# A gated cross-attention block with a quantised MLP on one Trainium2 core: an opening in four statistics groups, with four tiles normalised by GpSimd, and batch 1's tiles moved eight pieces later

## What is computed

```python
def xattn(features, textual_features, q_masks, Ws, W, w, b, Wcw, Wcb):
    txt_proj = einsum('btd,de->bte', textual_features, Ws)
    feat_proj = einsum('bfd,de->bfe', features, W)
    h = tanh(txt_proj[:, None, :, :] + feat_proj[:, :, None, :] + b)    # 2 x 2048 x 77 x 512
    rho = einsum('bftd,d->bft', h, w[:, 0]) + (1 - qm)[:, None, :] * NEG
    att = softmax(rho, axis=-1)
    txt_h = einsum('bft,btd->bfd', att, textual_features)
    return tanh(txt_h @ Wcw.T + bcw) * features + tanh(txt_h @ Wcb.T + bcb)

x = x + tanh(g_xattn) * xattn(layernorm(x), ...)
x = x + tanh(g_ffn) * ffn(layernorm(x), ...)     # silu(gate) * up, then down, operands quantised to 8 bits
```

## Time and profile before

| | us |
|---|---|
| median of 3 runs | 1372.93 (1372.75 to 1377.57) |
| profiled execution, its own time | 1375.13 |
| profiled execution, span from first to last instruction | 1373.2 |
| ACT busy | 1245.0 (91%) |
| DVE busy | 1166.2 (85%) |
| PE busy | 1117.5 (81%) |
| POOL busy | 14.0 (1%) |

### The profile page before, as it was taken

One profiled execution on the slowest core, in us unless ns is written; L12 is line 12 of the kernel. 1 busy time (PEld: TensorE's weight loads), 2 busy tenths in 40 slices (PEclk: granted clock), 3 DMA queues, 4 the chain that ended last, 5 costly groups with the idle time before them and its releaser, 6 DMA issues.

```text
span 1373.2 us, 16916 instructions
## 1 busy us (share of the span) xinstructions
PE 1117.5 (81%) x6941; PEld 353.4 (26%) x6963; DVE 1166.2 (85%) x1668; ACT 1245.0 (91%) x456; POOL 14.0 (1%) x32
## 2 busy tenths in 40 slices
PE   6888778788656787679889798787677779999998
PEld 5321112112111121112122122121111135444443
DVE  7688899986999889687999888777899967888776
ACT  4899999999899999999999999999999976555695
POOL 4000000000000000000000000000000000000000
PEclk9999899999899999899999999999998889999999
DMA  6000011100110001000000100000000004733196
GB/s 224 1 16 1 32 47 54 54 16 16 32 45 24 23 16 35 2 1 1 0 22 21 44 1 1 1 0 0 1 1 0 1 1 133 228 81 85 58 354 221
DMA packets 45107, 65.13 MB, mean 47 GB/s; under 512 B 19004, under 2 KB 21068, under 8 KB 45030
## 3 DMA queue, kind: packets, MB, share of 16 engines
q1 hardware_dynamic: 44128, 63.72, 14.6%
q10 hardware_dynamic: 197, 0.32, 0.1%
q0 software_dynamic: 704, 0.01, 0.0%
HBM read 46.20 MB, written 14.16 MB: 44 GB/s over the span
## 4 chain that ended last, share of the span: by engine, by line
ACT 76%; PE 19%; DVE 3%; DMA 1%; issue 1%; SPq 0%; DVEq 0%
ACT big L534 75%; PE ps L1241 10%; PE ps L1258 6%; PE ps L1047 1%; DMA wgu<-in_x_dram 1%; DVE big L733 1%; PE ps L1060 0%; ACT big L490 0%; PE ps L1218 0%; PE ps L1036 0%; PE ps L1104 0%; PE ps L1109 0%; DVE big L991 0%; SPq L336 0%; ACT big L527 0%
## 5 line engine op out<-in xcount | busy, mean ns | idle before, releaser
L534 ACT ACTIVATE big<-big 128x6144 f32<-128x6144 f32 x204 | 1056.7, 5268 | 5.8 <-DVE big L733 5.8
L733 DVE TENSOR_SCALAR big<-big,atxt 128x1536 f32<-128x1536 f32 (+2 forms) x915 | 794.1, 922 | 120.2 <-PE ps L1104 115.8
L1104 PE MATMUL ps<-big,wslide 128*32 128x512 f32 x4312 | 607.6, 621 | 193.8 <-ACT big L534 187.4
L1104 PEld LDWEIGHTS ps<-big,wslide 128*32 128x32 f32 x4312 | 131.5, 112 | 613.0 <-ACT big L534 318.6
L1047 PE MATMUL ps<-big,aux 128*128 128x512 f32 x256 | 144.9, 654 | 2.5 <-ACT big L476 1.6
L1241 PE MATMUL ps<-aux,wgu 128*128 128x512 bf16 x666 | 146.2, 379 | 0.7
L1109 PE MATMUL ps<-big,wslide 128*32 128x512 f32 x616 | 91.6, 710 | 39.3 <-ACT big L534 39.3
L579 ACT ACTIVATE aux<-ps,sgux 128x512 f32<-128x512 f32 x88 | 60.4, 687 | 69.0 <-PE ps L1241 66.3
L1241 PEld LDWEIGHTS ps<-aux,wgu 128*128 128x128 bf16 x680 | 66.4, 98 | 80.2 <-DMA aux<-aux 0.5
L991 DVE SCALAR_TENSOR_TENSOR big<-ps,sgux,aux 128x512 f32<-128x512 f32 x88 | 66.0, 750 | 17.8 <-PE ps L1241 13.4
L1258 PE MATMUL ps<-wd,wgu 128*128 128x512 bf16 x344 | 75.6, 379 | 0.4
(11 more groups left out here) (164 smaller groups left out, 398.9 us busy)
## 6 DMA issues: line engine op xcount, KB each, us to landing
aux<-in_x_dram SPq DMA_DIRECT2D x96, 256.0 KB, 2.8
out_dram<-aux SPq DMA_DIRECT2D x32, 256.0 KB, 3.9
hidden_spill<-big SPq DMA_DIRECT2D x6, 768.0 KB, 4.3
big<-hidden_spill SPq DMA_DIRECT2D x6, 768.0 KB, 7.0
wgu<-in_x_dram SPq DMA_DIRECT2D x11, 256.0 KB, 7.4
aux<-in_L_ffn_w_gate_dram SPq DMA_DIRECT2D x11, 256.0 KB, 2.7
aux<-in_L_ffn_w_up_dram SPq DMA_DIRECT2D x11, 256.0 KB, 3.0
aux<-in_L_ffn_w_down_dram SPq DMA_DIRECT2D x4, 704.0 KB, 4.0
```

Of the source, the lines that this page charges most:

```text
L534: nc.scalar.activation(unit, unit, ACT.Tanh).then_inc(tanh_done, 1)
L733: v.tensor_scalar(ring[:, place(p)], src, atxt[:, e, bt * T + t:bt * T + t + 1], None, ALU.add).then_inc(sums_ready, 1)
L1104: last = mm(bank(k)[32 * part:32 * part + 32, :], wslide[:, e, 31 - g:63 - g], unit[:, part * 512:(part + 1) * 512], start=(e == 0 and g = ...
```

## The change

- DVE's statistics of batch 0 come in four groups of four tiles; the last group of eight is cut in two, so the chain of 14 steps runs four times.
- Tiles 10, 11, 14 and 15 are normalised by GpSimd, with a semaphore of its own (`xn_pooled`), ahead of the mask's DMAs in its list.
- ACT copies tiles 8 to 11 before it takes part 1 of the first six pieces, copies part 2 of the projection itself, and takes pieces 6 to 8 in two halves of 3 x 1024 columns, both added by DVE (`half_sum`). PE is told of the first nine pieces one by one (`early_done`).
- PE projects part 2 whole before it transposes tiles 12 to 15, and the 24 small matmuls become 6, 8, 10 and 12 at four places.
- `TEXT_AT` is 8, 16, 24 in place of 2, 14, 26; `SPREAD_AT`, `CROW_AT`, `MASK_AT` are 15, 27, 80 in place of 18, 30, 82.
- `NORM_AT` starts at 172 in place of 164, and with it the maxima and `COPY_AT` of batch 1 (first copy on DVE at 185).
- The scores of batch 0 are copied out block by block at three pieces, and PE waits for one block at a time; `TSCORE_AT`, `SHIFT_AT` and `SUMS_AT` move with it.
- 30 small matmuls stand on PE before the last unit of twelve pieces; 100 become 140 and 28 become 34 behind the pieces.

The diff, cut to its core:

```diff
     UNIT_OF = [u for u, (_, n, _) in enumerate(UNITS) for _ in range(n)]
-    EARLY = 9
+    EARLY, FIRST = 9, 6
     KG = -(-T // 32)
...
         MAX0_AT = {12 + 4 * i: i for i in range(BT)}
-        TEXT_AT = {2 + 12 * (e - 1): e for e in range(1, EC)}
+        TEXT_AT = {8 + 8 * (e - 1): e for e in range(1, EC)}
         BIAS_AT = {later(at): e for at, e in TEXT_AT.items()}
-        SPREAD_AT, CROW_AT, MASK_AT = 18, 30, 82
+        SPREAD_AT, CROW_AT, MASK_AT = 15, 27, 80
         STATS_AT = {84 + 4 * i: i for i in range(BT)}
         CHAIN_AT = {148 + 2 * k: k for k in range(2)}
-        NORM_AT = {164 + 6 * i: i for i in range(BT)}
+        NORM_AT = {172 + 6 * i: i for i in range(BT)}
         MAX1_AT = {at + 2: i for at, i in NORM_AT.items()}
...
         WT_BYTES = [16 if kind == "d" else 32 for kind, _ in JOBS]
-        RHO_AT = {PER_B + 9: 0, LAST + 30: 1}
-        TSCORE_AT = {PER_B + at: (0, c) for c, at in enumerate((3, 6, 34, 40))}
-        TSCORE_AT.update({LAST + at: (1, c) for c, at in enumerate((42, 48, 100, 112))})
-        SHIFT_AT = {PER_B + at: (0, c) for c, at in enumerate((20, 26, 48, 54))}
+        RHO_AT = {PER_B + 9 + 6 * k: (0, k) for k in range(KG)}
+        RHO_AT.update({LAST + 30 + 4 * k: (1, k) for k in range(KG)})
+        TSCORE_AT = {PER_B + at: (0, c) for c, at in enumerate((18, 22, 40, 46))}
+        TSCORE_AT.update({LAST + at: (1, c) for c, at in enumerate((46, 52, 100, 112))})
+        SHIFT_AT = {PER_B + at: (0, c) for c, at in enumerate((32, 37, 54, 60))}
         SHIFT_AT.update({LAST + at: (1, c) for c, at in enumerate((84, 96, 140, 152))})
         EXP_AFTER = {UNIT_OF[at] + 1: f for at, f in SHIFT_AT.items()}
-        SUMS_AT = {PER_B + at: (0, c) for c, at in enumerate((62, 72, 82, 92))}
+        SUMS_AT = {PER_B + at: (0, c) for c, at in enumerate((66, 76, 86, 96))}
         SUMS_AT.update({LAST + at: (1, c) for c, at in enumerate((180, 204, 228, 252))})
...
               .then_inc(out_stored[n % 3], 16)
+
+        POOLED = (10, 11, 14, 15)
+
+        def wait_xn(engine, i):
+            if i in POOLED:
+                engine.wait_ge(xn_pooled, POOLED.index(i) + 1)
+            else:
+                engine.wait_ge(xn_ready, i + 1 - sum(k < i for k in POOLED))
...
+            for turn, tiles in ((2, POOLED[0:2]), (3, POOLED[2:4])):
+                pool.wait_ge(dve_chain, 14 * (turn + 1))
+                for i in tiles:
+                    nc.gpsimd.tensor_scalar(x_first(i), x_first(i), mean[:, i:i + 1], rstd[:, i:i + 1],
+                                            ALU.subtract, ALU.mult).then_inc(xn_pooled, 1)
+
             for part in range(Q4):
...
                     last = nc.scalar.activation(ring[:, t * S + part * 512:t * S + part * 512 + 512], feat[:, 0, cols], ACT.Tanh, bias=atxt[:, 0, t:t + 1])
-                    if part == Q4 - 1 and t % 3 == 2:
-                        last.then_inc(tanh_done, 1)
+                    if part == Q4 - 1:
+                        last.then_inc(early_done, 1)
...
                 copy_first(i)
-            early_tanh(0, 0, 6)
+            early_tanh(0, 0, FIRST)
             copy_feat_first(1)
-            early_tanh(1, 0, 6)
             for i in range(8, 12):
                 copy_first(i)
-            early_tanh(0, 6, EARLY)
-            early_tanh(1, 6, EARLY)
-            early_tanh(2, 0, 6)
-            early_tanh(3, 0, 6)
-            act.wait_ge(late_sums, 3)
-            rest = ring[:, 6 * S:9 * S].rearrange("p (t r) -> p t r", t=3)[:, :, 1024:S]
-            nc.scalar.activation(rest, rest, ACT.Tanh).then_inc(tanh_done, 1)
+            early_tanh(1, 0, FIRST)
+            copy_feat_first(2)
+            early_tanh(2, 0, FIRST)
+            held = ring[:, FIRST * S:EARLY * S].rearrange("p (t r) -> p t r", t=EARLY - FIRST)
+            act.wait_ge(half_sums, EARLY - FIRST)
+            nc.scalar.activation(held[:, :, 0:S // 2], held[:, :, 0:S // 2], ACT.Tanh)
+            early_tanh(Q4 - 1, 0, FIRST)
+            act.wait_ge(half_sums, 2 * (EARLY - FIRST))
+            nc.scalar.activation(held[:, :, S // 2:S], held[:, :, S // 2:S], ACT.Tanh).then_inc(early_done, EARLY - FIRST)
...
             def row_max(buf, i):
-                dve.wait_ge(xn_ready, i + 1)
+                wait_xn(dve, i)
                 return v.tensor_reduce(mxn[:, i:i + 1], buf, AX, ALU.max, apply_absolute_value=True)
...
                 for i in range(2 * g0, 2 * g1):
-                    normalise(x_first(i), i, turn)
+                    if i not in POOLED:
+                        normalise(x_first(i), i, turn)
...
             first_stats(2, 4, 1)
-            first_stats(4, BT // 2, 2)
+            first_stats(4, 6, 2)
+            first_stats(6, BT // 2, 3)
             for i in range(12, BT):
...
                  .then_inc(xnT_ready, 1)
-            for part in (2, 3):
-                dve.wait_ge(feat_ready, part)
-                dve.wait_ge(projected, part + 1)
-                move(feat[:, 0, part * 512:(part + 1) * 512], bank(FB[part % 2])).then_inc(feat_ready, 1)
-            dve.wait_ge(feat_ready, Q4)
+
+            def half_sum(half):
+                rows = slice(half * S // 2, (half + 1) * S // 2)
+                for t in range(FIRST, EARLY):
+                    v.tensor_scalar(ring[:, t * S:(t + 1) * S][:, rows], feat[:, 0, rows], atxt[:, 0, t:t + 1], None,
+                                    ALU.add).then_inc(half_sums, 1)
+
             dve.wait_ge(atxt_ready, 1)
-            for t in range(6, EARLY):
-                v.tensor_scalar(ring[:, t * S + 1024:(t + 1) * S], feat[:, 0, 1024:S], atxt[:, 0, t:t + 1], None,
-                                ALU.add).then_inc(late_sums, 1)
+            dve.wait_ge(feat_ready, 2)
+            half_sum(0)
+            dve.wait_ge(feat_ready, 3)
+            dve.wait_ge(projected, 4)
+            move(feat[:, 0, 3 * 512:S], bank(FB[1])).then_inc(feat_ready, 1)
+            dve.wait_ge(feat_ready, 4)
+            half_sum(1)
...
-            def soft_rho(bt):
+            def soft_rho(bt, k):
                 dve.wait_ge(scored, PER_B * (bt + 1))
-                for k in range(KG):
-                    v.tensor_scalar(rho_sb[:, k, :], bank(k), negm[:, k, bt:bt + 1], None, ALU.add).then_inc(rho_copied, 1)
+                v.tensor_scalar(rho_sb[:, k, :], bank(k), negm[:, k, bt:bt + 1], None, ALU.add).then_inc(rho_copied, 1)
...
             def transpose_rows(buf, i):
-                pe.wait_ge(xn_ready, i + 1)
+                wait_xn(pe, i)
                 if i >= 2:
...
-            def keep_warm(n):
+            def keep_warm(n, to=WB[0]):
                 for _ in range(n):
-                    mm(bank(WB[0])[:, 0:P], identb[:, :], identb[:, :], start=True, stop=True)
+                    mm(bank(to)[:, 0:P], identb[:, :], identb[:, :], start=True, stop=True)
...
             project(1)
-            keep_warm(24)
+            keep_warm(6)
             for i in range(8, 12):
                 transpose_rows(x_first(i), i)
-            for k in range(EC):
-                project(2, (k,))
-                transpose_rows(x_first(12 + k), 12 + k)
+            keep_warm(8)
+            project(2)
+            for i in range(12, BT):
+                transpose_rows(x_first(i), i)
+            keep_warm(10)
             project(3)
+            keep_warm(12)
             pe.wait_ge(wslide_ready, 1)
...
                 unit = ring[:, place(p)]
-                if p == UNITS[UNIT_OF[p]][0]:
-                    pe.wait_ge(tanh_done, UNIT_OF[p] + 1)
+                if p < EARLY:
+                    pe.wait_ge(early_done, p + 1)
+                elif p == UNITS[UNIT_OF[p]][0]:
+                    pe.wait_ge(tanh_done, UNIT_OF[p] + 1 - UNIT_OF[EARLY])
                 if p < LAST:
...
                     last.then_inc(sd_transposed, 1)
-                if p == PER_B:
-                    pe.wait_ge(rho_copied, KG)
+                if PER_B <= p < PER_B + T and (p - PER_B) % 32 == 0:
+                    pe.wait_ge(rho_copied, (p - PER_B) // 32 + 1)
                 if p == LAST:
...
                     transpose_scores(bt, c)
+                if p == UNITS[-3][0]:
+                    keep_warm(30, 0)
                 score(p)
...
-            keep_warm(100)
+            keep_warm(140)
             pe.wait_ge(max_spread, 1)
...
-            keep_warm(28)
+            keep_warm(34)
```

10 lines of the change are left out of this document (6 added, 4 removed).

## The result

The changed kernel takes 1365.41 us (median of 6 runs, 1363.74 to 1368.31), the kernel before, in turn with it, 1375.92 us (six runs, 1372.75 to 1381.54): a ratio of 0.9917, 95% interval 0.9898 to 0.9935, or 10.5 us less. The forecast was 10.3 us less, and 1362.6 us. The 2.8 us between that and 1365.41 come from the base: the three runs of before that were shown have a median of 1372.93, and with the three that followed it is 1375.92. Profiled, the span went from 1373.2 to 1363.1 us, the execution's own time from 1375.13 to 1364.92.

A forecast was written before the change was run, and what follows sets the result against it. ACT, with 76% of the span, was taken to bound the kernel. Hole -4.7, opening -5.6 and end 0 sum to -10.3 us, from the median 1372.93 to 1362.6 us; range 1361.0 to 1367.5.

The forecast's parts named there:

- What bounds the kernel: Whole kernel: ACT carries 76% of the span; gains ahead of 1119 us must come from ACT's idle time or work.
- the two places of the earlier trace: ACT's only idle places before 1119 us: 7.4 us between 24.00 and 55.70, 4.7 us between 342.60 and 358.10.
- the rival of DVE's list: Pieces 262 to 279, or PE's list at 20 to 30: ACT waits up to 1.9 + 1 us, 1365.5; chance 0.08.
- The hole, -4.7: At 342 us, first copy of batch 1: moved eight pieces later, DVE's wait for PE and ACT's waits end, -4.7 us.
- The opening, -5.6: Start up to ACT's first full unit: changed lists bring that unit at 50.1 in place of 55.70, -5.6 us.
- GpSimd's tile at 0.8 us: Opening: GpSimd normalises a tile in 0.8 us, so tile 10 is ready at 28.1, tile 11 at 28.9.
- The rival of a slow GpSimd: Opening: at 2.0 us a tile, tile 11 is ready at 32.3 and all behind comes 2.4 us later, 1365.0; chance 0.13.
- The clock rival: Opening: PE falls to 1.2 GHz all the same, projection 2 takes 7.4 us, +3.7 us, 1366.3; chance 0.14.
- The end, 0: Last units of pieces: 30 more small matmuls cost 1.0 us or nothing; bounds -0.5 to +1.0, taken as 0.
- Behind the pieces, -0.4: After the pieces: 140 small matmuls end PE's 2.63 us idle; next steps may run at a higher clock, some -0.4.
- The signs: Changed trace: first full unit at 50.1, PE clock 1.00 from 28 to 43 us, ACT without a gap to about 1109.
- The mask: Rival: GpSimd's 16 mask DMAs, moved later, come too late for piece 80; at 10 us each 1387.6; chance 0.05.

The follow-up runs named there:

- the shift alone: Kernel before with only NORM_AT at 172 in place of 164 (batch 1 normalisations eight pieces later): 1370.84 us against 1378.17, ratio 0.9945.
- GpSimd 14 and 15: Changed kernel with GpSimd normalising only tiles 14 and 15, DVE taking 10 and 11: 1364.97 us.

## Why the prediction was right, point by point

- **What bounds the kernel:** right. Most of what was gained is what ACT lost in the two places of the earlier trace rows. In the profiled run ACT has no wait from the first full unit to its last tanh, at pieces 262 to 279 either. So no cost of the moved tiles and weight jobs shows, and the rival of DVE's list is out.
- **The hole, -4.7:** right, with the mechanism as told. DVE's 7.91 us and ACT's 3.09 and 1.64 us go with the shift alone and come back without it. The stretch shrank by 5.0 to 5.1 us, 0.3 more than the two waits.
- **The opening, -5.6:** the size fits the pair by luck. The step that failed is GpSimd's tile at 0.8 us, between bounds of 0.48 and 2.4: it took 2.06 to 2.34, near the upper bound, and tile 11 was ready 9.75 us after the ninth statistic (29.46 - 19.71) in place of 28.9 - 22.09 = 6.8. The row it rested on, a conversion of 128 elements in 0.29 us, gives 2.4 us when it is taken four times for the elements and twice for the two operations, and that was nearest; what failed was to go down from there towards the time of another engine. Followed from the ninth statistic, the prediction gives 50.1 - 22.09 = 28.0 us, the kernel took 29.59, and with all tiles on DVE 28.41. So 1.2 of the 1.6 us are GpSimd's. The 2.38 us by which the ninth statistic came earlier covered this and more. The base was no better known: the same opening of before takes 31.59 us where the clock doesn't fall.
- **The rival of a slow GpSimd** had the duration right (2.0 us a tile) and the price wrong: 1.2 us, not 2.4. GpSimd began at 25.06, right behind the chain and beside DVE's tiles, not behind them, and the first copy of these tiles began 7.25 us after the ninth statistic (26.96 - 19.71) where I had 28.7 - 22.09 = 6.6, so ACT waited 1.25 us only. That its 1365.0 us lies nearer to the measured 1365.41 than the forecast does is chance: the base moved by 3 us.
- **The base of the opening.** I took 55.70 as the kernel's own. One execution's opening held one spell at 1.2 GHz; others have two, or none (31.59 to 35.81 us). A forecast of -5.6 against a sample with a spread of 4 us needed a word on it.
- **The clock rival** (0.14): right as a mechanism, +1.7 us and not +3.7 when it came in two of the variants, since the clock fell for part of the projection only (5.40 us without the small matmuls). That the 36 small matmuls mostly prevent it is what the times say.
- **The end, 0:** the case with the unit before at the lower clock was priced at +1.0 and measured +0.8, and it is what the profiled pair shows. The other case was told as "costs nothing" and gains 1.5: that the last forty fall below the full clock there was not in the earlier trace rows, which hold one case only.
- **Behind the pieces, -0.4:** right as a mechanism, with a size that stood on no row. PE idled 2.6 us ahead of the transposition at line 1193 in the four runs with 100 and 28 small matmuls, and 0.4 us in the ten with 140 and 34. From that transposition to the MLP's first wide projection (line 1241, now 1273) the four took 10.14 to 12.08 us at a mean granted clock of 0.71 to 0.83, the ten 9.67 to 9.89 us at 1.00. So the gain is 0.3 to 2.4 us; the two numbers were not changed alone. The stretch in the run with only the shift, then in the changed kernel:

```profile
1121.46:1133.54 12.08, 11.36 (x142) 10.52 (x144) 3.08 (x14) 7.03 (x11) 0.00 (x0) 0.72 0.36 91
```

```profile
1119.81:1129.70 9.89, 8.99 (x148) 8.43 (x150) 3.07 (x14) 6.98 (x11) 0.00 (x0) 1.00 0.40 119
```

To the end of the span the kernels of before took 252.7, 252.8, 254.5 and 254.6 us, the others 252.3 to 252.6 in nine runs of ten. The profiled run of the changed kernel was the tenth, 253.2, so that in the profiled pair this term came out as a loss of 0.55; there PE waited 0.8 us for DMA in the MLP.
- **The signs:** of those named, the wait of 1.1 us ahead of the wide tanh, the clock of 1.00, no wait of DVE at line 765 and ACT busy to about 1108 us came; the GpSimd tile of 0.8 us did not, and the first unit at 49.30 in place of 50.1 was better for the wrong reason.
- **The mask:** DVE never waited for it. That its DMAs no longer lie beside the loads of x was not counted in the prediction, which follows the lists from 22.09, "where nothing differs yet"; what it is worth is not settled. GpSimd issued the first twelve of its DMAs in 7.22 us, 0.60 us each, and the last four, beside DVE's second half sums and first full pieces, in 3.91 us, 0.66 to 1.39 each; with the kernel before these four took 2.06 us. So what the rival named may be there in small, but it needed 8 us each.

Taken over the executions, and not over one pair, the terms are about -5 for the shift, -2 to -4 for the opening (the difference being how often the clock falls), -0.3 to -2.4 behind the pieces, between +0.8 and -1.5 at the end, and 0 to about -1.2 for the earlier ninth statistic, which is not settled. The forecast's total was right; its division was not.

## What to carry to other kernels

A term that is read from one execution's opening has that execution's clock and arrivals in it: profile the same code twice before a difference of 2 us is called an effect of the list, and count from the last point at which both lists were alike. An operation that no row shows for an engine should be costed from a row of that engine, scaled by its elements and operations (here 2.4 us, measured 2.06 to 2.34), and not drawn towards the time that another engine takes for it (0.48). Then the question is whether the engine that does it now is full at all: DVE had the 2 us for the four tiles. Of fillers that are to hold PE's clock, those beyond the idle time of the slow case are paid for there (30 cost 0.8 us, twelve nothing); whether as few as twelve hold the clock in the other case is not shown.

## What the runs showed of the hardware

A normalisation of 128 x 512 float32 (subtract and multiply by a value per partition) takes GpSimd 2.06 us beside DVE's statistics and 2.34 us beside DVE's normalisations, and DVE 0.48 us. Two normalisations on DVE beside GpSimd's took 1.38 us in place of about 1.0. Statistics beside GpSimd kept their time (2.46 us for four), but the second step of the chain, a tensor_scalar on 128 x 4, took 0.52 in place of 0.17 us, and ended 0.04 us behind GpSimd's tile: 29.50 against 29.46. In the two runs in which GpSimd had no tile at that time (all tiles on DVE, and GpSimd 14 and 15) the same step took 0.17 us. With tiles 10 and 11 alone on GpSimd it took 0.52 us again:

```profile
28.13 2.06 POOL L468 TENSOR_SCALAR wd<-wd,mean,rstd 128x512 f32<-128x512 f32 x1
```

```profile
29.70 0.52 DVE L668 TENSOR_SCALAR mean<-mean 128x4 f32<-128x4 f32 x1
```

GpSimd's tile ends there at 30.19, DVE's step at 30.22. The Trainium skill ("SBUF — State Buffer", Who interferes with whom) says that a VectorE instruction of this kind, when it runs in a two-port mode, and one of GpSimd exclude each other for a whole instruction. In which mode these ran no trace shows; the small step agrees with it, while the two normalisations, which ended inside GpSimd's 2.34 us, do not show an exclusion for its whole length.

PE's clock took turns from unit to unit near the end of the pieces: 24 score matmuls took 2.78 us at a granted clock of 1.00, then 4.48 at 0.63, then 2.78 again, while ACT took about 5.2 us for each of these units. Which of the two falls on the unit before the last changed from execution to execution (the kernel before had 4.48 us there in one and 2.78 in the other), and without the 30 small matmuls the end changed with it by up to 1.5 us.
